# Eight chained attention and MLP layers on one core: norm statistics, reciprocal, row moves and output projections placed in other gaps of the attention slots

## What is computed

```python
# L0: x += attend(ln(x), causal); x += attend(ln(x), ctx); x += mlp(ln(x))
# L1: x += attend(ln(x), ctx)
# L2: x += attend(ln(x), mask);  x += attend(ln(x), ctx);  x += mlp(ln(x))
# L3: x += attend(ln(x), causal), 16 heads of 64
def _attend(q, k, v, causal):                # 16 heads of 16 numbers
    scores = jnp.einsum('bhqd,bhkd->bhqk', q, k) * scale
    if causal: scores = jnp.where(mask, scores, -jnp.inf)
    w = jax.nn.softmax(scores, axis=-1)
    return jnp.einsum('bhqk,bhkd->bhqd', w, v)
```

## Time and profile before

| | |
|---|---|
| median of three executions | 4353.77 us (4335.01 to 4356.31) |
| profiled execution, its own time | 4339.59 us |
| its span, first to last instruction | 4337.8 us |
| PE busy | 3924.7 us (90%) |
| DVE busy | 2729.8 us (63%) |
| ACT busy | 2393.4 us (55%) |
| POOL busy | 1656.3 us (38%) |
| mean clock granted to PE | 0.938 of full speed |

### The profile page before, as it was taken

How to read it: one execution, slowest core, us unless ns; L and a number is a source line. 1 busy time by engine, 2 the same in 40 slices (tenths; PEclk the granted TensorE clock), 3 DMA queues, 4 the chain that set the end, 5 groups by cost and what they waited for, 6 DMA issues and landing times. The chain is left out here.

```text
span 4337.8 us, 65569 instructions
## 1 busy us (share of the span) xinstructions
PE 3924.7 (90%) x20562; PEld 1981.6 (46%) x20562; DVE 2729.8 (63%) x6813; ACT 2393.4 (55%) x5093; POOL 1656.3 (38%) x1661
## 2 busy tenths in 40 slices
PE   6888899999796999999999999998897999999998
PEld 2334333333584333333333333333784555555555
DVE  4555567776565777788888877775663444444443
ACT  2445456666331666667777766666333555555553
POOL 2333321211331112137667631111324766666664
PEclk7889899999796999999999899999898999999999
DMA  4333334433002434333222244442000000000000
GB/s 97 85 65 68 71 72 96 84 73 58 18 1 39 106 79 82 70 65 74 59 54 58 51 81 88 78 78 52 21 1 29 6 11 11 1 11 11 11 6 10
DMA packets 135507, 220.34 MB, mean 51 GB/s; under 512 B 42736, under 2 KB 45168, under 8 KB 133488
## 3 DMA queue, kind: packets, MB, share of 16 engines
q1 hardware_dynamic: 135152, 216.02, 25.0%
HBM read 59.69 MB, written 5.51 MB: 15 GB/s over the span
## 5 line engine op out<-in xcount | busy, mean ns | idle before, releaser
L1035 ACT ACTIVATE prob<-ST 128x512 f32<-128x512 f32 (+3 forms) x2304 | 1168.8, 564 | 590.1 <-PE ST L596 581.5
L1252 DVE TENSOR_REDUCE mx<-MX 128x1 f32<-128x512 f32 x1536 | 957.1, 679 | 248.0 <-PE MX L596 247.2
L596 PE MATMUL MX<-stk 48*128 48x512 f32 (+3 forms) x2560 | 977.5, 456 | 119.5 <-DVE mx L1252 37.8
L596 PE MATMUL ST<-stk 50*128 50x512 f32 (+3 forms) x2560 | 987.8, 455 | 15.0 <-ACT prob L1035 10.9
L596 PEld LDWEIGHTS MX<-stk 48*128 48x128 f32 x2560 | 448.7, 195 | 792.4 <-DVE mx L1252 343.0
L596 PE MATMUL OUT<-prob,V 128*32 128x512 f32 (+3 forms) x5120 | 679.5, 604 | 62.5 <-POOL prob L1612 58.6
L1649 POOL TENSOR_SCALAR Pr<-Pr,mx 128x128 f32<-128x128 f32 (+3 forms) x512 | 548.3, 1083 | 386.3 <-DVE mx L1413 386.3
L596 PEld LDWEIGHTS ST<-stk 50*128 50x128 f32 x2560 | 445.3, 193 | 73.2 <-ACT prob L1035 39.1
L1245 DVE CUSTOM_DVE_ANT_0 MX<-MX,W_even 128x512 f32<-128x512 f32 x512 | 345.4, 704 | 73.8 <-PE MX L596 73.6
L1524 POOL CAST mhl<-mx 128x16 fp32r<-128x16 f32 x160 | 32.9, 205 | 934.9 <-DVE mx L1252 899.7
L1605 POOL TENSOR_TENSOR prob<-prob,W_odd 128x512 f32<-128x512 f32 x256 | 325.2, 1278 | 136.8 <-ACT prob L1035 135.6
(11 more groups left out here) (144 smaller groups left out, 6620.2 us busy)
## 6 DMA issues: line engine op xcount, KB each, us to landing
stk<-hi SPq DMA_DIRECT2D x640, 128.0 KB, 3.9
stk<-lo SPq DMA_DIRECT2D x320, 128.0 KB, 3.9
misc<-misc SPq DMA_DIRECT2D x160, 128.0 KB
sums<-spread SPq DMA_DIRECT2D x80, 256.0 KB
misc<-in_ctx_t SPq DMA_DIRECT2D x24, 512.0 KB, 6.1
W_even<-in_w SPq DMA_DIRECT2D x4, 1024.0 KB, 5.1
W_even<-in_w SPq DMA_DIRECT2D x2, 2048.0 KB, 9.1
XH<-in_ctx_rows SPq DMA_DIRECT2D x8, 512.0 KB, 4.4
```

The costliest lines, as they stand in the source:

```text
L596: return nc.tensor.matmul(o, l, r, start=start, stop=stop)
L1035: nc.scalar.activation(prob[:, k % 16:k % 16 + n_k, q0:S], STT[:, k % RING:k % RING + n_k, q0:S], ACT.Copy if addmask else ACT.Exp).then_i ...
L1252: nc.vector.tensor_reduce(m, MXT[:, k % RING:k % RING + n_k, :], AX.X, ALU.max).then_inc(mx_red, n_k)
```

## The change

It moves steps and splits one semaphore; the products themselves stay the same.

1. The statistics are taken two at a time behind runs 0 and 1, and combined behind run 2. POOL's `rows_scale` stands behind the second `clear` (or `add_mask`) instead of before it.
2. `few` and `raw` have semaphores of their own. In SP's queue the move of `few` stands behind the stack of the keys and ahead of that of `raw`, and the stack of the queries stands behind both and behind the maxima's rows. At the end of a slot `few` is moved ahead of the maxima's rows.
3. DVE's reciprocal stands behind run 3 instead of 2 (in SELF2 behind 4 instead of 3), and waits for `few` alone. POOL's product waits for `raw` too.
4. O0 and O1 stand whole in gaps 7 and 9 of even slots (before: 8, 9 and 10), V0 and V1 in gaps 7 and 9 of odd slots (before: 6, 8, 9), M0 in gap 8 (before: 7). The sum of O1 into x is taken in the same slot instead of the next.

```diff
             def slot(u, c, b, p, on):
-                         ("V0", half == 1 and on["a"]), ("M0", on["m"]), ("V1", half == 1 and on["a"]),
-                         ("O0", half == 0 and on["op"]), ("O1", half == 0 and on["op"]),
+                         ("V0", half == 1 and on["a"]), ("O0", half == 0 and on["op"]), ("M0", on["m"]),
+                         ("V1", half == 1 and on["a"]), ("O1", half == 0 and on["op"]),
...
                     if on["stack1"]:
-                        for kind in range(2):
-                            stack(U + 1, 1 - half, 1, kind)
+                        stack(U + 1, 1 - half, 1, 0)
                     if on["tail"]:
-                        move(U - 1, 1 - half, 1, GB - 1 + half)
+                        move_few(U - 1, 1 - half, 1)
+                        move_raw(U - 1, 1 - half, 1, GB - 1 + half)
                     if on["b"]:
                         max_rows(U, half, 1)
+                    if on["stack1"]:
+                        stack(U + 1, 1 - half, 1, 1)
...
+                    if on["b"]:
+                        move_few(U, half, 0)
                     if on["m"]:
                         max_rows(U + 1, 1 - half, 0)
                     if on["b"]:
-                        move(U, half, 0, GB)
+                        move_raw(U, half, 0, GB)
...
-                def move(U, half, g, GBu):
+                def move_few(U, half, g):
                     waits(sp, (ov_evac, 2 * U + g + 1),
-                          (at_ready, BASE + U - 1))
+                          (spread_out, 16 * (U - 1)))
+                    sp.dma_start(few[64 * g:64 * g + 64, half, :], ovs[1:P:32, g, :].rearrange("h (c n) -> h c n", n=32)).then_inc(few_in[g], 16)
+                def move_raw(U, half, g, GBu):
+                    wait(sp, at_ready, BASE + U - 1)
                     if GBu > 0:
                         sp.wait_ge(l_full, out_job(GBu - 1) + 1)
-                    sp.dma_start(raw[64 * g:64 * g + 64, half, :], ovs[0:P:2, g, :]).then_inc(ov_moved[g], 16)
-                    sp.dma_start(few[64 * g:64 * g + 64, half, :], ovs[1:P:32, g, :].rearrange("h (c n) -> h c n", n=32)).then_inc(ov_moved[g], 16)
+                    sp.dma_start(raw[64 * g:64 * g + 64, half, :], ovs[0:P:2, g, :]).then_inc(raw_in[g], 16)
...
-                        if half == 1 and on["a"] and r == 6:
-                            begin(u, "V0")
+                        if half == 1 and on["a"] and r in (7, 9):
+                            begin(u, "V0" if r == 7 else "V1")
                             for t in range(2):
-                                project_values(wq(sa, 2), source, 0, t)
-                        if on["m"] and r == 7:
-                            begin(u, "M0")
-                            turn_max(U + 1, 1 - half, 0)
...
+                                project_values(wq(sa, 2), source, (r - 7) // 2, t)
+                        if half == 0 and on["op"] and r in (7, 9):
+                            if r == 7:
                                 pe.wait_ge(at_ready, BASE + 2 * GB)
...
+                                project_out(se, (r - 7) // 2, t)
+                        if on["m"] and r == 8:
+                            begin(u, "M0")
+                            turn_max(U + 1, 1 - half, 0)
...
-                        if u != -2 and norm is not None and r < 4:
+                        if u != -2 and norm is not None and r < 2:
...
-                            statistics(NB * sn + bn, xt(bn, r), r)
-                            if r == 3:
-                                combine(NB * sn + bn)
-                        if half == 1 and r == 0 and sums_of(s, u):
-                            output_sum(end_of(s, u - 1, b), out_job(GB - 1), 1)
-                        if on["tail"] and r == (3 if lagged(s, u) else 2):
+                            for t in (2 * r, 2 * r + 1):
+                                statistics(NB * sn + bn, xt(bn, t), t)
+                        if u != -2 and norm is not None and r == 2:
+                            combine(NB * norm[0] + norm[1])
+                        if on["tail"] and r == (4 if lagged(s, u) else 3):
                             invert(U, 1 - half)
...
+                        if half == 0 and on["op"] and r in (7, 9):
+                            output_sum((se, be), L_NO[s, u, "O0" if r == 7 else "O1"], (r - 7) // 2)
+                        if half == 1 and on["a"] and r in (7, 9):
+                            values_out(sa, u, 1 - par, (r - 7) // 2)
...
                     for g in range(2):
-                        dve.wait_ge(ov_moved[g], 32 * U)
+                        dve.wait_ge(few_in[g], 16 * U)
...
                         add_mask(u, U, 0)
-                    if norm is not None:
-                        rows_scale(N)
                     if clears:
                         clear(U, 1)
                     if adds:
                         add_mask(u, U, 1)
+                    if norm is not None:
+                        rows_scale(N)
...
                     if on["tail"]:
+                        for g in range(2):
+                            pool.wait_ge(raw_in[g], 16 * U)
                         pool.wait_ge(spread_in, 16 * U)
```

More of the change, by code:

```diff
@@ L197, in program @@
         pv_done, ov_evac = sem("pv_done"), sem("ov_evac")
-        ov_moved = [sem("ov_moved0"), sem("ov_moved1")]
+        few_in, raw_in = [sem("few_in0"), sem("few_in1")], [sem("raw_in0"), sem("raw_in1")]
         recip_done, at_ready = sem("recip_done"), sem("at_ready")
@@ L665, in slot @@
                                 project(wq(sa, 0), half, hT, cc)
-                        if half == 1 and on["a"] and r == 6:
-                            begin(u, "V0")
+                        if half == 1 and on["a"] and r in (7, 9):
+                            begin(u, "V0" if r == 7 else "V1")
                             for t in range(2):
-                                project_values(wq(sa, 2), source, 0, t)
-                        if on["m"] and r == 7:
+                                project_values(wq(sa, 2), source, (r - 7) // 2, t)
+                        if half == 0 and on["op"] and r in (7, 9):
+                            if r == 7:
+                                pe.wait_ge(at_ready, BASE + 2 * GB)
+                            begin(u, "O0" if r == 7 else "O1")
+                            for t in range(2):
+                                project_out(se, (r - 7) // 2, t)
+                        if on["m"] and r == 8:
                             begin(u, "M0")
                             turn_max(U + 1, 1 - half, 0)
-                        if half == 1 and on["a"] and r in (8, 9):
-                            if r == 8:
-                                begin(u, "V1")
-                            project_values(wq(sa, 2), source, 1, r - 8)
-                        if half == 0 and on["op"] and r in (8, 9):
-                            if r == 8:
-                                pe.wait_ge(at_ready, BASE + 2 * GB)
-                                begin(u, "O0")
-                            project_out(se, 0, r - 8)
-                        if half == 0 and on["op"] and r == 10:
-                            begin(u, "O1")
-                            for t in range(2):
-                                project_out(se, 1, t)
                         if half == 1 and r == 10 and norm_of(s, u) is not None:
@@ L1025, in product_out @@
                     act.wait_ge(pv_done, 8 * U + 4 * (g + 1))
-                    wait(act, ov_moved[g], 32 * U)
+                    wait(act, few_in[g], 16 * U)
+                    wait(act, raw_in[g], 16 * U)
                     nc.scalar.activation(ovs[:, g, :], OUT[:, :], ACT.Copy).then_inc(ov_evac, 1)
```

6 lines of the change are left out of this document (removed).

## The result

The changed kernel takes 4219.1 us (median of four executions, 4215.9 to 4221.2), beside 4353.6 us for the kernel before on the same chip: a ratio of 0.970, 95% interval 0.967 to 0.973. The forecast was 4200 us, between 4135 and 4270. The profiled execution took 4215.89 us against 4339.59, so 123.7 us less, where the sum of the prediction had 142.5.

A forecast was written before the change was run, and what follows sets the result against it. PE, fed by the other engines, was taken as the bound, with time to win in SELF0 and SELF2. 80 + 38 + 36 - 4 - 7.5 = 142.5 us off 4339.59 gives 4197, stated as 4200 us, range 4135 to 4270.

The forecast's parts named there:

- the stall of SELF0: SELF0 odd slots: PE's values wait for POOL's `clear`, 58.6 us in 8 times; ending it wins 80 us.
- the chain: SELF0 odd slots: late `few` holds DVE's reciprocal, then the combining, POOL's second `clear` and PE, idle 8.12 us.
- the stall and what follows it: SELF0 odd slots: the remaining 10.9 us between M1 and M0 beyond V0's time, of which 0.9 stays unrecovered.
- the 0.6 for O0: SELF0 even slots: O0, a run earlier, waits 0.6 us for POOL's product, 4 us in 7 slots.
- the 0.5 for the stack: SELF0: the queries' stack, moved later, costs 0.5 us at tile 16 in each of 15 slots, 7.5 us.
- the ring of three tiles: Part 4's moved jobs, all stages: PE may be three tiles ahead, so the rest was costed at nothing.
- I take 1.6 us in each of 24 odd slots: Crossing stages: gain from odd slots' extra time over even ones, less V0's 1.99 us; 38 us in all.
- The chain is the same: SELF2: POOL idles before the norm and ACT for POOL's mask, as in SELF0; ending it wins 36 us.
- Rival 4: Slower: the queries' stack arrives late at tile 16 in every slot; 4400 us, chance 0.04.
- The reciprocal cannot hold DVE again: SELF0 odd slots: `few`, issued earlier, lands by about 311.0 us, when the later reciprocal stands there too.
- The 4.4 us that the sum kept for `few`: SELF0 odd slot: time `few` needed from issue to DVE's reciprocal, read from the timeline before the change.
- Rival 2: It wins more, since the clock stays up in SELF0 and SELF2: 213 us, so 4127 us, chance 0.06.

The follow-up runs named there:

- mixed: Changed kernel; SELF0 even slots with gaps of before; SELF2 with M1 earlier, K split over gaps 2 and 3, V0, V1, O0, O1 and M0 moved; 4137.6 us, ratio 0.952.
- no_part4: Changed kernel with all the gaps of before, so parts 1 to 3 alone; 4218.7 us, ratio 0.9689 against the kernel before.
- recip_and_queries: Changed kernel with the reciprocal behind run 2 (SELF2: 3) and the queries' stack ahead of `few`, both as before; 4216.3 us, ratio 0.9706.
- recip_early: Changed kernel with the reciprocal behind run 2 (SELF2: 3) as before, still waiting for `few` alone; 4221.9 us, ratio 0.9705.

## Why the prediction was right, and where it was not

The total, 123.7 us by the profiled executions against 142.5, is right by one term and by the luck of two errors: crossing stages 37 us better than their term, SELF2 62 us worse.

**Right, the stall of SELF0.** Eight odd slots went from a mean of 38.0 to 27.4 us, 10.6 each where I had 10.0. The third `clear` is late by 0.6 us (I left 0.9). The experiments confirm both causes of the chain: taking back the norm's place costs 54 us, taking back `few` and the reciprocal 26. Part of the gain is the clock: 0.88 over the 498 us of SELF0 before is 120 us at the lower level, 0.95 over 425 us is 42, and half of the difference, by this estimate up to 39 of the 73 us, comes with it. The sum had this inside "the stall and what follows it"; that was a reading of whole slots, which held. The even slots went from 27.8 to 29.5 us: 1.7 us each, not the 0.6 for O0 and the 0.5 for the stack. Gap 7, with O0, takes 5.51 us there. M1 to M0 is 18.9 us in the mean of eight odd and 20.6 of seven even slots, 1.7 apart, within the 2 us named; the clock is 0.96 in the window of the earlier trace rows and 0.95 in SELF0's own slots, so it is at the edge of the forecast "above 0.95".

**Under-sized, the crossing stages: 38 us forecast, 75.3 measured, above the bound of 65.** The step that failed is part 4, which gave 43 us and which I had at nothing: "The gaps 7 and 9 take two jobs of 2 us each instead of 8, 9 and 10 ... I cost the rest at nothing: PE has its cover in the ring of three tiles". Parts 1 to 3 gave 32.6 us. The term for them, "I take 1.6 us in each of 24 odd slots", makes 34 us in the 21 odd slots measured, so its size is right, but by luck: it is a difference between odd and even slots and takes the even ones for clean. They were not. The reciprocal waited in all 14 slots of CROSS0, and the gain came as 0.8 us in every slot, even and odd. CROSS0's even slots take 30.2 us before and 28.8 after.

**Wrong, SELF2: -36 us forecast, +26 measured.** Two steps failed. The first is the same sentence on the ring: in SELF2 gaps 7 and 9 hold the values as well, which the kernel's text tells; 4 us at the lower clock behind 1 to 2 us of values is more than the ring covers, and DVE, busy for 529 of 620 us, is what must not wait. That is 33 to 48 us. The second is "The chain is the same": it is, but in this kernel's SELF2 other work of PE and DVE, gap 3 above all, took its time anyway, so its removal gave 7 to 11 us with the gaps of before and 21.5 with part 4's. In mixed, with gap 3 split, part 1 is worth 36.6 us, near the 36 of the sum; that is another kernel than the one forecast. That gap 3 was the longest could have been read from the timeline before the change.

**Right or harmless.** Rival 4, late query stacks, is worth 0.9 us of waits and nothing in time. "The reciprocal cannot hold DVE again" is right, with one wait of 1.1 us in SELF0, and was over-provided, since either half would do. The 4.4 us that the sum kept for `few` were too much: with the change the last count of its second half's semaphore comes 1.8 us after the issue in the median. Rival 2 was half right: the clock rose to 0.95 in SELF0 by the stalls' end alone, but in SELF2 parts 1 to 3 left it at 0.90 (no_part4), and it took the split of gap 3 and the norm's new place together to bring it from 0.91 to 0.97 or 0.98.

## What to carry to other kernels

Where PE fills gaps between tiles that a slower engine paces, weigh each gap with all that stands in it, in each stage by that stage's own table: in SELF2 a gap longer than what the ring holds was lost time for the pacing engine, and a short one next to it did not give it back. A stall's removal is worth what remains after the other work that lies over it: in SELF2 the end of POOL's stall was worth from 7 to 36.6 us, by what stood in the gaps around it. And read a slot's cost whole, not as a difference to a neighbour taken for clean.

## What the hardware showed beyond that

How long after its issue a transfer is usable depends on what is ahead of it. In recip_and_queries `few` stands behind six stacks, with a semaphore that nothing else raises, and the reciprocal that waits for it alone starts 5.1 us after the issue:

```profile
254.13 0.62 SPq L519 DMA_DIRECT2D few<-misc  x1
259.27 0.35 DVE L1263 RECIPROCAL few<-few 128x32 f32<-128x32 f32 x1 [1.94 <-DMA few<-misc]
```

Over its 60 slots with such a wait the median from issue to reciprocal is 4.9 us, and 1.85 the least. The counts of the semaphore of this second half of `few` in the trace tell the same: over 80 issues the first comes 1.1 us after the issue in the median, the last only after 4.7. With three stacks in front of it and, in the median, 2.3 us between them and it (recip_early, the reciprocal as early), the first comes after 1.0 and the last after 1.8, and only 8 slots wait. The Trainium skill (DMA: Bandwidth & Descriptors, section on queues, rings and completion order) says that the count rises on a DMA engine only behind all earlier writes of that engine. The runs agree with it; the mechanism itself no row shows.
